# Experts' input stored as rows in halves, gate made in the experts' stage, an expert pair's y summed in one bank, nine weight blocks loaded early

## The chip, the cores and the metric

The kernel runs on one core of a Trainium2 chip. The metric is device time in microseconds (us) of one execution; lower is better. TensorE (PE) does the matmuls, VectorE (DVE), ScalarE (ACT) and GpSimd (POOL) the elementwise work, and SyncE (SP) issues the DMA transfers.

## What is computed

128 sequences of 128 tokens, width 256, run through four residual stages. Only the second one, a mixture of experts, and the LayerNorm ahead of it are touched by the change in what they do.

```python
x = x + cross_attention(layernorm(x), ctx)         # 16 heads of 16
x = x + ffn_moe(layernorm(x), Wg, bg, W1, b1, W2, b2)
x = x + attention2(ctx, ctx, layernorm(x), mask)   # 16 heads
x = x + spiking_ffn(layernorm(x))                  # 256 -> 1024 -> 256, 5 steps

def ffn_moe(x, ...):
    gate_logits = x @ Wg + bg                      # 8 experts
    top_vals, top_idx = top_k(gate_logits, 2)
    gate_scores = softmax(top_vals)                # per token
    for i in range(2):
        e = top_idx[..., i].reshape(-1)[:batch]    # one expert per sequence
        h = gelu(x @ W1[e] + b1[e])                # 256 -> 1024
        y = h @ W2[e] + b2[e]                      # 1024 -> 256
        out = out + gate_scores[..., i:i+1] * y
```

`reshape(-1)[:batch]` takes the first 128 entries, so all experts' numbers come from the 128 tokens of the first sequence: sequence b uses the two experts of token b of sequence 0.

## The kernel before

A unit is a pair of sequences (`PAIR` = 2), and there are 64 units. Products are made in f16 halves: every operand is a high part and a low part, and `three_passes` (L181) adds hi·hi, hi·lo and lo·hi, the matmuls of L183, L184 and L185. A shape like 128x512 in a row of a matmul is rows by columns of the result.

There are four phases, with a preparation of weights ahead of each. In a phase each engine runs its own list of `(lag, task)`, written out by hand: in step s, `run_steps` (L122) lets every task work on unit s − lag, in the order of the list, and an engine takes its instructions strictly in that order. The pieces of PSUM banks are shared out by a `plan` (lag, name) in the same order.

**Phase 1**, `attention(first=True)` (L470 to L1171): cross attention, then the LayerNorm for the experts. POOL makes the factors (`rstd1`: L397, L401, L412, L416), ACT applies them (`norm1`, L422), TensorE transposes the result (`t_1`, L449 in `transpose_pair`), ACT and DVE make its halves (`hi_h`, `lo_h`), and SP stores them column by column in `h_scratch` (`store_h`). TensorE makes the gate logits (`gate`, 14 matmuls of 8 columns), ACT copies them, DVE takes the largest (`top`); the experts' numbers of unit 0 are written to `idx_scratch` by SP once all units are done. From unit 32 on, every four units, SP loads one of four blocks (512 KB) of expert weights into `region` (`ahead`, L597). POOL's other tasks are `norm0` (factors L397, L401, then L440), `bias_x` (L771) and `maxima` (L744 to L749, small).

**Preparation of phase 2** (`prepare_experts`, L1240): 32 blocks of weights; ACT makes the high part of each (L1279), DVE the low part (L1285), from eight slots of raw blocks; the last six are done behind the shared heads' part (`prepare_shared_heads`). `gates` (L1174) makes the softmax of all gates at once.

**Phase 2**, `experts` (L1311): a unit has 8 chunks n (which sequence a, which of its two experts, which half of the hidden width). `up(n)` makes 4 groups of 128 hidden columns with 2 x 3 matmuls of 128 columns each (L183 to L185); `down(n − 3)` makes 4 steps j, in each one matmul of 512 columns (L1466: the high part of the hidden values against both halves of W2 side by side) and one of 256 (L1468: the low part against the high half). An expert's result thus stands in one bank of 512 columns as two sums, which DVE adds with two further operations (`add`, L1558, four per sequence). Between up and down ACT applies gelu (L1495) and DVE splits (L1513, L1516).

The expert's number is a value in a register, read from memory at the start of each unit on every engine that needs it (`read`, L1306), and each address that depends on it is computed by register instructions of the engine's sequencer, ahead of the matmul. In the profile these are `FUSED_REGOPS` and `ALU_OP` on PEldq, the read is `TENSOR_LOAD`. The lines of `down`:

```python
for j in range(4):
    row = w["w2"][:, bass.ds(e, 1), 4 * half + j, :, :].rearrange("p o t n -> p (o t n)")
    pe.matmul(o[:, :], hh[n % NH][:, j, :], row, start=half == 0 and j == 0, stop=False, ...)
    m = pe.matmul(o[:, 0:D], hl[n % NH][:, j, :], row[:, 0:D], start=False, stop=half == 1 and j == 3, ...)
```

**Phase 3**, `attention(first=False)`: the same function, second attention. It stores its LayerNorm as rows in halves (`rows1`, L430 and L433 in `split_rows`, on POOL) and **phase 4**, `spiking` (L1693), reads them with a transposing DMA (`columns_in`, L461 to L463). Phase 3's `ahead` loads late weights.

Of the kernel before, what the change touches and what calls it, by code (L numbers as in the profile page):

```python
# [36 lines left out]
P = 128  # L37
# [17 lines left out]
M_X = 15  # L55
KEPT = 3e38
# [143 lines left out]
def constants(k):  # L200
# [6 lines left out]
    c["minus_half"] = k.sb("minus_half", [P, PAIR], F32)  # L207
    s = k.sem("s_const")
# [3 lines left out]
    def gpsimd(g):  # L212
# [8 lines left out]
        g.memset(c["minus_half"][:, :], -0.5)  # L221

# [247 lines left out]
def attention(nc, k0, c, w, io, n_seq, first, glog_top=None, idx_d=None, raw_ahead=()):  # L470
# [9 lines left out]
    with ExitStack() as ctx:  # L480
# [22 lines left out]
        hT = first and two("hT", [P, 2, KB, PAIR * S], F16)  # L503
        hr = first or two("hr", [P, PAIR, 2, D], F16)
        gl = two("gl", [P, PAIR, EXP], F32)
        g8 = two("g8", [P, PAIR, EXP], F32)
        i8 = k.sb("i8", [P, EXP], U32)
# [24 lines left out]
        s_y2, s_yh, s_yl, s_o, s_x1, s_t1, s_hh, s_hl = (g(n) for n in "s_y2 s_yh s_yl s_o s_x1 s_t1 s_hh s_hl".split())  # L532
        s_g, s_gl, s_g8, s_gt = g("s_g"), g("s_gl"), g("s_g8", PAIR), g("s_gt")
        s_cut, s_x = ({n: g(f"s_{what}{n}") for n in cut_by} for what in ("cut", "under"))
        s_xb, s_hrh, s_hr = g("s_xb"), g("s_hrh"), g("s_hr")
        s_idx, s_idxd, s_late = k.sem("s_idx"), k.sem("s_idxd"), k.sem("s_late")

        if first:
            plan = [(10, "t_1"), (7, "y1"), (3, "v"), (8, "o"), (2, "t_x"), (7, "t_y"), (10, "gate"), (2, "q"),
                    (1, "t_c"), (6, "y0"), (2, "k"), (4, "t_max")]  # L540
            shared = (("t_1", "t_x", "y0", "t_max"), ("y1", "v", "t_y", "t_c"), ("o", "gate", "q", "k"))
# [39 lines left out]
        with nc.Block() as block:  # L581
            @block.sync
            def _(sp):
# [35 lines left out]
                def store_h(u):  # L619
                    if not first:  # L620
                        s_hr.wait(sp, u)
                        d_h.inc(rows_out(sp, h_out[u.no], hr[u.slot][:, :, :, :]), u)
                        return
                    s_hl.wait(sp, u)
                    s_hh.wait(sp, u)
# [1322 lines left out]
```

## Time and profile before

| | us |
|---|---|
| median of 3 executions | 3932.9 (3925.84 to 3933.43) |
| the profiled execution | 3932.82 |
| its span in the trace | 3930.9 |
| phase 1, first to last L401 of the first norm | 28.0 to 909.7 |
| phase 2, first to last read of the experts' numbers | 1039.1 to 2418.4 |
| phase 4's first load | 3244.5 |

| engine | busy us | share of the span | instructions |
|---|---|---|---|
| PE | 3732.9 | 95% | 47650 |
| PEld | 2907.6 | 74% | 47650 |
| DVE | 3129.4 | 80% | 5333 |
| ACT | 2251.2 | 57% | 4658 |
| POOL | 1879.8 | 48% | 2866 |

PE is a matmul, PEld the load of its stationary operand, which overlaps it. Ends of matmuls are modelled: a busy PE is not one at its peak. Register instructions and reads (PEldq) are not counted as busy; they have start times of their own in the trace. A row gives the line of the program, the engine, the operation, the tile written and those read, and how many; then durations in ns (min/median/max) and the first and last start in us.

### The profile page before, as it was taken

How to read it: one execution, taken by the hardware profiler on the slowest of the kernel's cores; microseconds unless marked ns; L12 is line 12 of the kernel's file. 1: busy time of each engine (PE TensorE's matmuls, PEld its weight loads, DVE VectorE, ACT ScalarE, POOL GpSimd, SP SyncE). 2: the span in 40 equal slices, each digit the busy share in tenths (PEclk: the TensorE clock that was granted, in tenths of full speed). 3: DMA queues.
4: the chain of work that ended last, by engine and by line, in shares of the span. 5: the costliest groups of instructions: out<-in, count | busy, mean ns of one | idle time of the engine just before them, and what ended most of it. 6: DMA issues, size and time to landing. Idle time of an engine off the chain costs nothing. (4 is left out here: it accounts for less than half of the span.)

```text
span 3930.9 us, 134664 instructions
## 1 busy us (share of the span) xinstructions
PE 3732.9 (95%) x47650; PEld 2907.6 (74%) x47650; DVE 3129.4 (80%) x5333; ACT 2251.2 (57%) x4658; POOL 1879.8 (48%) x2866
## 2 busy tenths in 40 slices
PE   5999999998499999999999997899999989999999
PEld 4788888886377777777777775466666658888888
DVE  4899998997777777777777775699888976777777
ACT  3777777776544444444444443577667764555554
POOL 4555555553133332222222223366666666777776
PEclk9999999999699999999999998899999999999999
DMA  4666666664522222222222223699999962233232
GB/s 118 184 193 193 199 200 200 192 193 126 192 77 84 77 80 64 73 67 70 73 64 76 62 75 78 152 214 212 203 218 212 217 151 71 73 79 76 73 81 68
DMA packets 766624, 502.33 MB, mean 128 GB/s; under 512 B 194421, under 2 KB 740408, under 8 KB 765864
## 3 DMA queue, kind: packets, MB, share of 16 engines
q1 hardware_dynamic: 765064, 493.22, 47.8%
q8 instruction: 420, 6.88, 0.8%
q14 instruction: 212, 1.74, 0.2%
q0 software_dynamic: 928, 0.49, 0.1%
HBM read 268.05 MB, written 214.96 MB: 123 GB/s over the span
## 5 line engine op out<-in xcount | busy, mean ns | idle before, releaser
L1495 ACT ACTIVATE phase_loop_hf<-phase_loop_hid,phase_b1T 128x128 f32<-128x128 f32 x2048 | 586.0, 368 | 706.1 <-PE phase_loop_hid L185 677.0
L183 PE MATMUL phase_loop_hid<-phase_loop_moe_h,phase_w_hi 128*128 128x128 f16 x4096 | 728.6, 220 | 12.0 <-DMA phase_loop_moe_h<-h_scratch 12.0
L185 PE MATMUL phase_loop_hid<-phase_loop_moe_h,phase_w_lo 128*128 128x128 f16 x4096 | 726.7, 219 | 0.0
L184 PE MATMUL phase_loop_hid<-phase_loop_moe_h,phase_w_hi 128*128 128x128 f16 x4096 | 726.7, 219 | 0.0
L1131 DVE TENSOR_REDUCE phase_loop_mx<-phase_loop_score 128x8 f32<-128x1024 f32 x512 | 625.5, 1222 | 102.7 <-PE phase_loop_score L868 92.1
L1466 PE MATMUL phase_loop_moe_y<-phase_w,phase_loop_hh 128*128 x2048 | 693.6, 379 | 1.1
L1468 PE MATMUL phase_loop_moe_y<-phase_w,phase_loop_hl 128*128 x2048 | 558.2, 273 | 0.0
L1042 ACT ACTIVATE phase_loop_pt<-phase_loop_scoreT 128x1024 f32<-128x1024 f32 x448 | 459.2, 1025 | 169.6 <-PE phase_loop_scoreT L902 169.2
L183 PEld LDWEIGHTS phase_loop_hid<-phase_loop_moe_h,phase_w_hi 128*128 x4096 | 400.7, 98 | 86.4 <-issue 12.3
L397 POOL TENSOR_SCALAR phase_loop_ln0b_ve<-phase_loop_ln0b_mv 128x2 f32<-128x2 f32 x64 | 23.1, 361 | 918.4 <-DVE phase_loop_ln0b_mv L390 918.4
L1513 DVE TENSOR_SCALAR phase_loop_hh<-phase_loop_hf 128x512 f16<-128x512 f32 x512 | 259.2, 506 | 250.2 <-PE phase_loop_moe_y L1468 196.8
L1516 DVE SCALAR_TENSOR_TENSOR phase_loop_hl<-phase_loop_hf,phase_loop_hh 128x512 f16<-128x512 f32 x512 | 411.4, 804 | 17.6
L184 PEld LDWEIGHTS phase_loop_hid<-phase_loop_moe_h,phase_w_hi 128*128 x4096 | 401.6, 98 | 5.7
L1827 POOL TENSOR_TENSOR phase_loop_sp_q<-phase_loop_sp_r 128x512 f32<-128x512 f32 x256 | 330.7, 1292 | 155.7 <-ACT phase_loop_sp_r L1798 155.7
L185 PEld LDWEIGHTS phase_loop_hid<-phase_loop_moe_h,phase_w_lo 128*128 x4096 | 400.7, 98 | 0.1
L1782 PE MATMUL phase_loop_sp_yb<-all_region,phase_loop_sp_fh 128*128 128x256 f16 x2048 | 349.2, 273 | 1.3 <-POOL phase_loop_sp_fl L1733 1.3
L1466 PEld LDWEIGHTS phase_loop_moe_y<-phase_w,phase_loop_hh 128*128 128x128 f16 x2048 | 200.2, 98 | 190.6 <-issue 4.1
L933 PE MATMUL phase_loop_av<-phase_loop_pt,phase_loop_vx 128*32 128x128 f32 x8192 | 332.6, 280 | 3.3 <-ACT phase_loop_pt L1042 3.2
L1798 ACT ACTIVATE phase_loop_sp_r<-phase_loop_sp_hid 128x512 f32<-128x512 f32 x256 | 153.1, 598 | 317.7 <-PE phase_loop_sp_hid L185 301.4
L1851 DVE SCALAR_TENSOR_TENSOR phase_loop_sp_cnt<-phase_loop_sp_y,phase_loop_sp_cnt 128x512 f32<-128x512 f32 x256 | 320.4, 1252 | 8.8
L183 PE MATMUL phase_loop_sp_hid<-phase_loop_sp_h,all_region 128*128 128x256 f16 x1024 | 280.4, 274 | 15.0 <-DMA phase_loop_sp_h<-h_scratch 15.0
L184 PE MATMUL phase_loop_sp_hid<-phase_loop_sp_h,all_region 128*128 128x256 f16 x1024 | 280.5, 274 | 0.0
(255 smaller groups left out, 9421.2 us busy)
## 6 DMA issues: line engine op xcount, KB each, us to landing
qk_scratch<-phase_loop_qk SPq DMA_DIRECT2D x192, 256.0 KB, 3.2
phase_loop_qS<-qk_scratch SPq DMA_DIRECT2D x768, 64.0 KB, 3.0
phase_loop_cin<-in_ctx SPq DMA_DIRECT2D x128, 256.0 KB, 4.2
x_scratch<-phase_loop_x SPq DMA_DIRECT2D x128, 256.0 KB, 3.7
phase_loop_kS<-qk_scratch SPq DMA_DIRECT2D x384, 64.0 KB, 2.5
ks_scratch<-ct_scratch SPq DMA_DIRECT2D x384, 64.0 KB, 2.4
phase_loop_kS<-ks_scratch SPq DMA_DIRECT2D x128, 192.0 KB, 3.9
phase_loop_xin<-in_x SPq DMA_DIRECT2D x64, 256.0 KB
```

The lines of the kernel that those rows point to most:

```text
L183: eng.matmul(out, l_hi, r_hi, start=start, stop=False)
L184: eng.matmul(out, l_hi, r_lo, start=False, stop=False)
L185: return eng.matmul(out, l_lo, r_hi, start=False, stop=stop)
L933: m = pe.matmul(av_bank[32 * j:32 * j + 32, ch * S:(ch + 1) * S], vx[u.slot4][:, a, 2 * b + hh, :], pt[n % len(pt)][:, hh * CH + j, :], st ...
L1042: act.activation(pt[n % len(pt)][:, :, :], score_t_bank[:, :].rearrange("p (j n) -> p j n", j=HB2), ACT.Exp, scale=exp_scale).then_inc(s_e ...
L1131: v.tensor_reduce(to, score_bank[:, :].rearrange("p (h j n) -> p h j n", h=2, j=CH), AX.X, ALU.max).then_inc(s_mx.sem, 1)
L1466: pe.matmul(o[:, :], hh[n % NH][:, j, :], row, start=half == 0 and j == 0, stop=False, skip_group_check=True)
L1468: m = pe.matmul(o[:, 0:D], hl[n % NH][:, j, :], row[:, 0:D], start=False, stop=half == 1 and j == 3, skip_group_check=True)
L1495: i = act.activation(hf[n % NF][:, j, :], hid_bank[n % 4][:, j * S:(j + 1) * S], ACT.Gelu, bias=w["b1"][:, bass.ds(e * HB + (4 * half + j) ...
L1516: v.scalar_tensor_tensor(out=hl[n % NH][:, :, :], in0=hf[n % NF][:, :, :], scalar=p2(H_X), in1=hh[n % NH][:, :, :], op0=ALU.mult, op1=ALU. ...
L1782: m = pe.matmul(o, l[n % 4][:, j, at], rr[:, hb, :], start=st and i == 0, stop=sto and i == 2, skip_group_check=True)
L1827: g.tensor_tensor(q[n][:, :, :], r[n][:, :, :], r[n][:, :, :], ALU.mult).then_inc(s_q.sem, 1)
```

## The change

- Phase 1 no longer makes h in columns. `rows1` runs on POOL in this phase too, right behind `rstd1` of the same unit, and `store_h` stores rows. `t_1`, `hi_h`, `lo_h`, `gate`, `copy_gate` and `top` are gone, and all five task lists and the banks' plans of the phase are written in another order. Nine weight blocks, not four, are loaded ahead, every three units (phase 3's late loads follow the same divisor). Nothing is written to `idx_scratch` at the end.
- The preparation reads the first unit's h with a transposing load, makes its gate logits, finds the experts' numbers after nine low parts and writes them to `idx_scratch` before block 26. It has 13 slots. `gates` is gone.
- Phase 2 reads h with `columns_in`, makes the gate logits of each unit on TensorE at the unit's start (`gate_logits`), their two largest on DVE behind the first split (`top`), and the softmax on POOL in five small operations (`gates`, two of them powers).
- In `down` each j has three matmuls of 256 columns, all into the same 256 columns; both experts of a sequence have the two halves of one bank. DVE adds twice per sequence, not four times. Several buffers move to a part of `region`.

```diff
-                        o = y_bank[a][ex]
+                        o = y_bank[a][:, ex * D:(ex + 1) * D]
                         for j in range(4):
                             row = w["w2"][:, bass.ds(e, 1), 4 * half + j, :, :].rearrange("p o t n -> p (o t n)")
-                            pe.matmul(o[:, :], hh[n % NH][:, j, :], row, start=half == 0 and j == 0, stop=False,
-                                      skip_group_check=True)
-                            m = pe.matmul(o[:, 0:D], hl[n % NH][:, j, :], row[:, 0:D], start=False,
-                                          stop=half == 1 and j == 3, skip_group_check=True)
+                            high, low = hh[n % NH][:, j, :], hl[n % NH][:, j, :]
+                            pe.matmul(o, high, row[:, 0:D], start=n % 4 == 0 and j == 0, stop=False, skip_group_check=True)
+                            pe.matmul(o, high, row[:, D:2 * D], start=False, stop=False, skip_group_check=True)
+                            m = pe.matmul(o, low, row[:, 0:D], start=False, stop=n % 4 == 3 and j == 3, skip_group_check=True)
...
-                tasks = [(1, read), (2, read_last)]
+                def gate_logits(u):
+                    d_h.wait(pe, u)
+                    s_gl.wait(pe, u.back(1))
+                    gate_products(pe, gate_bank, late, c, hT[u.slot]).then_inc(s_g.sem, 1)
+
+                tasks = [(1, read), (2, read_last), (1, gate_logits)]
...
-                        for i in range(4):
-                            ex, part = i // 2, i % 2
...
+                        for ex in range(2):
...
-                run_steps(g, [(2, factors), (2, rows), (2, bias), (2, halves)], units, 3)
+                run_steps(g, [(1, gates), (2, factors), (2, rows), (2, bias), (2, halves)], units, 3)
...
-                    d_h.inc(sp.dma_start(hT[u.slot][:, :, :, :], io["h"][u.no]), u)
+                    d_h.inc(columns_in(sp, hT[u.slot][:, :, :, :], io["h"][u.no]), u)
...
-                    tasks = [(9, rstd1), (2, norm0), (3, bias_x), (4, maxima)]
+                    tasks = [(6, bias_x), (8, maxima), (5, norm0), (12, rstd1), (12, rows1)]
...
-                    tasks = [(4, score(0)), (6, av(0)), (10, make["t_1"]), (7, make["y1"]), (6, av(1)), (4, score(1)),
...
+                    tasks = [(3, make["t_x"]), (8, make["t_y"]), (7, av(2)), (5, score(3)), (7, score_t(3)),
...
-                    n, at = divmod(u.no - units // 2, 4)
-                    if n not in range(4) or at:
+                    n, at = divmod(u.no - units // 2, 3)
+                    if n not in range(len(raw_ahead) if first else 4) or at:
...
+            if i == len(jobs) - LAST:
+                sp.wait_ge(s_gv, 3)
+                sp.dma_start(idx_d, which[0:idx_d.shape[0], 0:2]).then_inc(s_id, 16)
+                sp.wait_ge(s_id, 16)
+                sp.dma_start(listed[:, :, :], idx_d.rearrange("(o u a) n -> o u (a n)", o=1, a=PAIR)).then_inc(s_i, 16)
...
-        low(v, range(len(jobs) - LAST))
+        low(v, range(EARLY))
+        v.wait_ge(s_gp, 1)
+        v.tensor_scalar(logits[:, :], gate_bank[:, 0:EXP], p2(-LN_X - W_X), None, ALU.mult).then_inc(s_gv, 1)
+        v.wait_ge(s_gv, 1)
+        v.max(best[:, :], logits[:, :]).then_inc(s_gv, 1)
+        v.wait_ge(s_gv, 2)
+        v.max_index(which[:, :], best[:, :], logits[:, :]).then_inc(s_gv, 1)
+        low(v, range(EARLY, len(jobs) - LAST))
```

Here is TensorE's program in phase 2, the last trio of an up and the first step of the down behind it, before. ISA is the form of register instruction that the profile calls FUSED_REGOPS, REGISTER_ALU is its ALU_OP; `w` is the experts' weights, `hh` and `hl` the hidden values' halves.

```order
L183 ISA
L183 MATMUL phase_loop_hid<-phase_loop_moe_h,phase_w_hi 128x128
L184 MATMUL phase_loop_hid<-phase_loop_moe_h,phase_w_hi 128x128
L185 REGISTER_ALU
L185 MATMUL phase_loop_hid<-phase_loop_moe_h,phase_w_lo 128x128
L1466 ISA
L1466 MATMUL phase_loop_moe_y<-phase_w,phase_loop_hh 128x512
L1468 MATMUL phase_loop_moe_y<-phase_w,phase_loop_hl 128x256
```

And the same place now (the lines of `three_passes` are one further down, `hh` and `hl` stand in `region`):

```order
L184 ISA
L184 MATMUL phase_loop_hid<-phase_loop_moe_h,phase_w_hi 128x128
L185 MATMUL phase_loop_hid<-phase_loop_moe_h,phase_w_hi 128x128
L186 REGISTER_ALU
L186 MATMUL phase_loop_hid<-phase_loop_moe_h,phase_w_lo 128x128
L1452 ISA
L1452 MATMUL phase_loop_moe_y<-phase_w,all_region 128x256
L1453 ISA
L1453 MATMUL phase_loop_moe_y<-phase_w,all_region 128x256
L1454 MATMUL phase_loop_moe_y<-phase_w,all_region 128x256
```

A step j of down has one register instruction and 768 columns in two matmuls before, and two register instructions and the same 768 columns in three matmuls now. Over the program TensorE has 6144 ISA before and 8192 now, and 4096 REGISTER_ALU in both.

This is POOL's program in phase 1, one step, before:

```order
L401 TENSOR_TENSOR phase_loop_ln1a_rs<-phase_loop_ln1a_ve,all_minus_half 128x2
L412 TENSOR_SCALAR phase_loop_ln1a_nm<-phase_loop_ln1a_mv 128x2
L416 TENSOR_TENSOR phase_loop_ln1a_nb<-phase_loop_ln1a_nm,phase_loop_ln1a_rs 128x2
L397 TENSOR_SCALAR phase_loop_ln0a_ve<-phase_loop_ln0a_mv 128x2
L401 TENSOR_TENSOR phase_loop_ln0a_rs<-phase_loop_ln0a_ve,all_minus_half 128x2
L440 TENSOR_SCALAR phase_loop_ln0a_xn<-phase_loop_xin,phase_loop_ln0a_mv,phase_loop_ln0a_rs 128x256 x2
L771 TENSOR_TENSOR phase_loop_xin<-phase_loop_xin,phase_bo_b 128x512
L744 TENSOR_SCALAR phase_loop_nm<-phase_loop_mx 128x32
```

And now:

```order
L401 TENSOR_SCALAR phase_loop_ln1a_ve<-phase_loop_ln1a_mv 128x2
L405 TENSOR_TENSOR phase_loop_ln1a_rs<-phase_loop_ln1a_ve,all_minus_half 128x2
L416 TENSOR_SCALAR phase_loop_ln1a_nm<-phase_loop_ln1a_mv 128x2
L420 TENSOR_TENSOR phase_loop_ln1a_nb<-phase_loop_ln1a_nm,phase_loop_ln1a_rs 128x2
L434 CAST phase_loop_hr<-phase_loop_ln1a_xn 128x2x256
L437 TENSOR_TENSOR phase_loop_hr<-phase_loop_ln1a_xn,phase_loop_hr 128x2x256
L761 TENSOR_TENSOR phase_loop_xin<-phase_loop_xin,phase_bo_b 128x512
L734 TENSOR_SCALAR phase_loop_nm<-phase_loop_mx 128x32
```

L434 reads ln1a_xn, which ACT makes from the nb of L420, the instruction just ahead of it on POOL. Behind the two new operations stand the bias and the maxima of later steps.

## Rows read from the trace of the kernel before

**Rows 1.** Stretches: us, busy PE, PEld, DVE, ACT, POOL (x count), PEclk, DMA, GB/s

```profile
150.00:900.00 750.00, 748.70 (x11717) 604.19 (x11707) 675.68 (x1383) 551.11 (x906) 393.31 (x798) 1.00 0.66 195
1100.00:2350.00 1250.00, 1249.03 (x14850) 989.17 (x14848) 976.96 (x1857) 594.03 (x1972) 349.19 (x509) 1.00 0.24 72
```

**Rows 2.** First phase, line L401: ns min/median/max, first to last start, forms

```profile
L401 POOL TENSOR_TENSOR phase_loop_ln0a_rs<-phase_loop_ln0a_ve,all_minus_half x64: 712/713/725, 28.0 to 909.7; 128x2 f32<-128x2 f32 x64
```

**Rows 3.** First phase, TensorE, lines L449 and L185, one unit

```profile
L449 PE MATMUL phase_loop_ring<-all_ident,phase_loop_ln1a_xn x4: 272/273/328, 500.7 to 501.0; 128*128 128x128 f32 x4
...
L185 PE MATMUL phase_loop_ring<-phase_wg_hi,phase_loop_hT x4: 166/166/167, 507.6 to 507.9; 128*128 128x8 f16 x4
```

**Rows 4.** POOL groups, one period, 509.8:524.1; busy, mean ns, idle before, releaser

```profile
L744 POOL TENSOR_SCALAR phase_loop_nm<-phase_loop_mx 128x32 f32<-128x32 f32 x2 | 0.6, 301 | 7.8 <-DVE phase_loop_mx L1131 7.8
...
L397 POOL TENSOR_SCALAR phase_loop_ln1a_ve<-phase_loop_ln1a_mv 128x2 f32<-128x2 f32 x1 | 0.2, 191 | 1.2 <-DVE phase_loop_ln1a_mv L390 1.2
```

**Rows 5.** Third phase's last units: POOL L430, L433 and ACT L422

```profile
L430 POOL CAST phase_loop_hr<-phase_loop_ln1b_xn x2: 608/608/609, 3237.1 to 3238.9; 128x512 f16<-128x512 f32 x2
...
L433 POOL TENSOR_TENSOR phase_loop_hr<-phase_loop_ln1b_xn,phase_loop_hr x2: 1151/1152/1152, 3237.8 to 3239.7; 128x512 f16<-128x512 f32 x2
...
L422 ACT ACTIVATE phase_loop_ln1b_xn<-phase_loop_x,phase_loop_ln1b_nb,phase_loop_ln1b_rs x2: 584/592/599, 3237.2 to 3237.7; 128x256 f32<-128x256 f32 x2
```

**Rows 6.** Last norm factor of a phase, and first work or load behind it

```profile
L416 POOL TENSOR_TENSOR phase_loop_ln1a_nb<-phase_loop_ln1a_nm,phase_loop_ln1a_rs x2: 194/194/195, 974.1 to 976.8; 128x2 f32<-128x2 f32 x2
...
L1279 ACT ACTIVATE phase_w_hi<-all_region x8: 1040/1056/1058, 988.1 to 1030.2; 128x1024 f16<-128x1024 f32 x8
...
L416 POOL TENSOR_TENSOR phase_loop_ln1b_nb<-phase_loop_ln1b_nm,phase_loop_ln1b_rs x1: 196/196/196, 3236.9 to 3236.9; 128x2 f32<-128x2 f32 x1
...
L463 SPq DMA_TRANSPOSE phase_loop_sp_h<-h_scratch x2: 1256/1274/1292, 3244.5 to 3245.8; - x2
```

**Rows 7.** Preparation, DVE line L1285: first, last, and those around the break

```profile
L1285 DVE SCALAR_TENSOR_TENSOR phase_w_lo<-all_region,phase_w_hi x8: 1211/1226/1226, 990.0 to 1031.8; 128x1024 f16<-128x1024 f32 x8
...
L1285 DVE SCALAR_TENSOR_TENSOR phase_w<-prep_expert_raw,phase_w x8: 1216/1224/1226, 995.7 to 1037.5; 128x1024 f16<-128x1024 f32 x8
...
L1285 DVE SCALAR_TENSOR_TENSOR phase_w<-all_region,phase_w x2: 1216/1221/1226, 1025.2 to 1033.0; 128x1024 f16<-128x1024 f32 x2
```

**Rows 8.** Second phase's first matmuls, and the fourth phase's after a transposing load

```profile
L183 PEldq FUSED_REGOPS  x64: 46/46/46, 1041.7 to 1059.6; - x64
...
L183 PE MATMUL phase_loop_sp_hid<-phase_loop_sp_h,all_region x3: 393/421/421, 3248.3 to 3249.6; 128*128 128x256 f16 x3
```

**Rows 9.** Reads of the experts' numbers by TensorE's sequencer, whole run

```profile
L1306 PEldq TENSOR_LOAD <-phase_idx x65: 782/817/1016, 1039.1 to 2418.4; - x65
```

**Rows 10.** L183, the first chunk of a unit, then the second

```profile
L183 PEldq FUSED_REGOPS  x8: 46/46/46, 1320.2 to 1321.8; - x8
...
L183 PE MATMUL phase_loop_hid<-phase_loop_moe_h,phase_w_hi x8: 219/223/228, 1320.5 to 1322.0; 128*128 128x128 f16 x8
...
L183 PEldq FUSED_REGOPS  x8: 46/46/46, 1322.6 to 1324.5; - x8
...
L183 PE MATMUL phase_loop_hid<-phase_loop_moe_h,phase_w_hi x8: 219/219/219, 1323.5 to 1324.7; 128*128 128x128 f16 x8
```

**Rows 11.** Register instructions of up (L185) and of down (L1466) in one chunk

```profile
L185 PEldq ALU_OP  x8: 32/32/32, 1301.3 to 1303.0; - x8
...
L1466 PEldq FUSED_REGOPS  x4: 46/46/60, 1300.6 to 1301.0; - x4
```

**Rows 12.** Page, groups: down's two matmuls

```profile
L1466 PE MATMUL phase_loop_moe_y<-phase_w,phase_loop_hh 128*128 x2048 | 693.6, 379 | 1.1
L1468 PE MATMUL phase_loop_moe_y<-phase_w,phase_loop_hl 128*128 x2048 | 558.2, 273 | 0.0
```

**Rows 13.** POOL line L404, norm factors in the second phase

```profile
L404 POOL TENSOR_TENSOR phase_loop_ln0b_rv<-phase_loop_ln0b_ve,all_minus_half x64: 722/1175/1178, 1076.0 to 2427.6; 128x2 f32<-128x2 f32 x64
```

**Rows 14.** One stretch of the third phase, columns as in rows 1

```profile
2805.00:2810.00 5.00, 5.00 (x45) 3.38 (x45) 1.63 (x3) 2.51 (x4) 2.14 (x4) 0.50 1.17 179
```

More of the change, by code:

```diff
@@ L55 @@
 M_X = 15
+AHEAD = 9
 KEPT = 3e38
@@ L502, in attention @@
         x1 = two("x1", [P, PAIR, D], F32)
[L503 to L507, printed above, removed]
+        hr = two("hr", [P, PAIR, 2, D], F16)
         qkd = [nc.dram_tensor(f"qk_scratch{int(first)}{i}", (4, D, PAIR * S), F16, kind="Internal").ap() for i in range(2)]
@@ L619, in store_h @@
                 def store_h(u):
[L620 to L625, printed above, removed]
-                    d_h.inc(sp.dma_start(h_out[u.no], hT[u.slot][:, :, :, :]), u)
+                    s_hr.wait(sp, u)
+                    d_h.inc(rows_out(sp, h_out[u.no], hr[u.slot][:, :, :, :]), u)
                 def store_ct(u):
@@ L1171, in _, with gate_products @@
                 run_steps(v, tasks, units, DEPTH)
-def gates(kk, top, gate, n_seq):
-    e, d = kk.sb("gate_e", [P, n_seq], F32), kk.sb("gate_d", [P, n_seq], F32)
-    s = kk.sem("s_gate")
-    def vector(v):
-        v.tensor_tensor(d[:, :], top[:, :, 1], top[:, :, 0], ALU.subtract).then_inc(s, 1)
-        v.wait_ge(s, 2)
-        v.tensor_scalar(d[:, :], e[:, :], 1.0, None, ALU.add).then_inc(s, 1)
-        v.wait_ge(s, 3)
-        v.reciprocal(d[:, :], d[:, :]).then_inc(s, 1)
-        v.wait_ge(s, 4)
-        v.tensor_scalar(gate[:, :, 0], d[:, :], p2(-H_X - W_X), None, ALU.mult).then_inc(s, 1)
-        v.wait_ge(s, 5)
-        v.tensor_tensor(gate[:, :, 1], gate[:, :, 0], e[:, :], ALU.mult)
-    def scalar(act):
-        act.wait_ge(s, 1)
-        act.activation(e[:, :], d[:, :], ACT.Exp).then_inc(s, 1)
-    return {"vector": vector, "scalar": scalar}
+def gate_products(pe, bank, w, c, hT):
+    hi, lo = w["wg"]
+    for a in range(PAIR):
+        out = bank[:, a * EXP:(a + 1) * EXP]
+        at = slice(a * S, (a + 1) * S)
+        for kb in range(KB):
+            three_passes(pe, out, hT[:, 0, kb, at], hT[:, 1, kb, at], hi[:, kb, :], lo[:, kb, :], kb == 0, False)
+        m = pe.matmul(out, c["ones10"][:, 0:S], w["bg"][:, :], start=False, stop=True)
+    return m
 def late_views(region):
@@ L1308, in read_experts, with experts @@
     return values
-def experts(nc, k0, c, w, late, io, n_seq, gate):
+def experts(nc, k0, c, w, late, io, n_seq, spare):
     units = n_seq // PAIR
@@ L1530, in weight, with top @@
                 def weight(u, a, ex):
-                    return gate[:, bass.ds(u.no * PAIR + a, 1), ex]
+                    return gate[u.slot][:, a, ex:ex + 1]
+                def top(u):
+                    s_g.wait(v, u)
+                    s_gates.wait(v, u.back(2))
+                    settle(v, ln.ticks_v)
+                    v.tensor_scalar(gl[u.slot][:, :, :], gate_bank[:, 0:PAIR * EXP].rearrange("p (a n) -> p a n", a=PAIR),
+                                    p2(-LN_X - W_X), None, ALU.mult).then_inc(s_gl.sem, 1)
+                    s_gl.wait(v, u)
+                    for a in range(PAIR):
+                        v.max(g8[u.slot][:, a, :], gl[u.slot][:, a, :]).then_inc(s_g8.sem, 1)
                 def add_bias(a):
@@ L1910, in build @@
                 kk = Kit(nc, tmp, "prep2", k2)
-                most, rest = prepare_experts(kk, c, w, io, idx_d, first_raw, s_first)
-                together(nc, gates(kk, top, gate, n_seq), most, prepare_shared_heads(kk, c, w_late, io), rest)
-            experts(nc, k2, c, w, w_late, io, n_seq, gate)
+                most, rest = prepare_experts(kk, c, w, w_late, io, idx_d, first_raw, s_first)
+                together(nc, most, prepare_shared_heads(kk, c, w_late, io), rest)
+            experts(nc, k2, c, w, w_late, io, n_seq, region[:, 4 * HID:AHEAD * HID])
             k2.end_phase()
```

172 lines of the change are left out of this document (86 added, 86 removed).

## The prediction

> **What bounds the kernel now.** First I read the busy times of two long stretches [rows 1]. TensorE is busy for 748.70 of 750 us in the first phase and for 1249.03 of 1250 in the experts' (second) phase, at a granted clock of 1.00, the upper of its two levels (2.4 GHz). VectorE follows with 675.68 and 976.96. So both phases seem to be TensorE's. But a busy PE is a modelled number, and next I asked what hands TensorE its work.
>
> In the experts' phase each address depends on a number read at run time, so register instructions stand between the matmuls. Read the starts. In the first chunk of a unit the eight L183 matmuls start from 1320.5 to 1322.0 us, 1.5 / 7 = 0.21 us apart; in the next chunk from 1323.5 to 1324.7, 0.17 apart [rows 10]. A trio (L183 to L185) of 128-column matmuls can thus go in 0.17 us, and in the first chunk it does not. In that chunk the sequencer's own register instructions (PEldq) are as far apart as the matmuls: eight from 1320.2 to 1321.8, 0.23 each. With one more (ALU_OP) in each trio, eight of which take 1301.3 to 1303.0, 0.24 each [rows 11], a register instruction costs the sequencer about **0.12 us**. In down, four of them stand from 1300.6 to 1301.0, 0.13 apart though two matmuls lie between each pair [rows 11]: the register instruction is the price, the matmuls pass for nothing.
>
> Now count a unit. The reads of the experts' numbers stand (2418.4 - 1039.1) / 64 = **21.55 us** apart [rows 9], 0.9 us of which is the read (817 ns, and the way to the next instruction). The sequencer handles 8 chunks of 16 + 4 = 20 register instructions: 160 x 0.12 = 19.2, and 0.9, and some 1.4 of waits and hiccups. TensorE's arithmetic needs 24 x 0.057 (a third of 0.17) in up. In down the 512-column matmul lasts 379 ns and the 256-column one 273 [rows 12], an 8-column one 166 [rows 3]: the columns cost about 0.213 and 0.107, together 0.32 per j and 1.28 per chunk. The sum is 2.65 per chunk, 21.2 per unit. **Sequencer and arithmetic are level, and there is no slack in the sequencer.** That is the finding on which the forecast hangs.
>
> **The change, part by part.** The profiled execution took 3932.82 us (its span is 3930.9), the median of the runs is 3932.9, so the sum starts from 3932.8.
>
> *First phase.* TensorE loses the transposes of h (four L449 matmuls from 500.7 to 501.0, 0.5 with the last one's own time) and the gate (14 matmuls of 8 columns from 507.5, the last of the L185 kind starting at 507.9, 0.4) [rows 3]. A unit takes (909.7 - 28.0) / 63 = 14.00 us now [rows 2], TensorE-bound, so 13.1 after: 64 x 0.9 = 57.6, taken as **-57**. ACT and DVE only lose work here. POOL gains rows1: 0.61 for the cast and 1.15 for the subtraction [rows 5] with some 0.2 between; and, since it stands right behind rstd1 of the same unit, the wait for ACT's norm1: factor done at 3237.1 (3236.9 [rows 6] and 0.2), xn done at 3237.7 + 0.6 = 3238.3 [rows 5], 1.2 us. POOL now idles 7.8 / 2 + 1.2 = 5.1 of 14.0 us [rows 4] (the 7.8 counts two units). Occupied: 8.9 + 2.0 + 1.2 = 12.1 of 13.1. It fits by 1.0 us; what is queued behind the wait is bias_x and maxima, for which there are two or more steps of lag. Cost 0.
>
> *Phase ends.* From the last norm factor to the first work of the preparation: 988.1 - 976.8 = 11.3 us, through transposes, hi, lo, gate and the write and wait for the experts' numbers. In the third phase, which stores rows as the change does, from factor to the next phase's load are 3244.5 - 3236.9 = 7.6 [rows 6]. With 0.6 for what lies between load and work: **-3**.
>
> *Preparation.* DVE makes 32 low parts; the first starts at 990.0, the last ends at 1037.5 + 1.2 = 1038.7: 48.7 us. Between the 26th, which ends at 1025.2 + 1.2 = 1026.4, and the 27th at 1031.8 stand 5.4 us for the shared heads; the last six take 1038.7 - 1031.8 = 6.9, or 1.15 each, while the 26 before, which had to wait for their blocks, took 1026.4 - 990.0 = 36.4, or 1.40 each [rows 7]. With nine blocks ahead and thirteen slots I expect the pace of the last six: 32 x 1.15 + 5.4 + 0.6 for the first unit's top = 42.8. Between no gain and -7 (no addition for the top), taken at **-6**, since the blocks that waited are the ones now ahead. The first h comes by a transposing load beside this, and the experts' numbers are written before block 26.
>
> *Start of the second phase.* From the read at 1039.1 [rows 9] to the first instruction at 1041.7 [rows 8] are 2.6 us. A transposing load takes longer: issue at 3244.5 [rows 6], matmul at 3248.3 [rows 8], 3.8. That is +1.2, and +0.4 for the gate ahead of the first chunk [rows 3], less what the sequencer does meanwhile: **+1.5**. Later units load two units ahead, which hides it.
>
> *Gate in the unit.* 14 matmuls, 0.4 us of arithmetic per unit, no register instructions. Where the sequencer is the bound TensorE has holes for them: 0; where not, 64 x 0.4 = 26. POOL's five small operations hold two powers of up to 1.18 us [rows 13]; with the rest about 3 us per unit, beside the 349.19 / 1250 x 21.55 = 6.0 of now [rows 1]. They start after chunk 0 and are wanted after chunk 5, 12 us later: 0. The row shows the same power at 0.71 us in the first phase [rows 2] and 1.18 here: something holds POOL up. The Trainium skill (SBUF — State Buffer, section "SBUF: two separate sides") says that GpSimd and VectorE share a port pair as an exclusive lock, which would fit the row and leave the sum as it is; no trace here tells it from other causes.
>
> *Down.* Per j one 512-column and one 256-column matmul become three of 256. The columns are the same, 2 x 0.107 for 0.213: 0. But the sequencer now computes an address for the second matmul too: 8 rather than 4 register instructions per chunk, 32 more in a unit. At 0.118 (half of 0.236) that is 3.8 us per unit, and the sequencer had nothing left: 21.55 + 3.75 = **25.3**, so 64 x 3.75 = **+240**. Lower bound: the shortest chunk, 1322.6 - 1320.2 = 2.4 [rows 10], eight times, + 0.9 + 3.8 + 0.2 = 24.1, +163. Upper: every register instruction at the present mean, (21.55 - 0.9) / 160 = 0.129, 192 of them + 0.9 + 0.4 for the gate = 26.1, +291. DVE loses two of four adds per sequence there, and is far from the bound.
>
> Third and fourth phase: late weight loads stand three units apart, not four; one such load costs a hole and a stretch at half clock (0.50 [rows 14]), and their number stays four: 0.
>
> Sum: 3932.8 - 57 - 3 - 6 + 1.5 + 240 = 4108.3, forecast **4108**.
>
> **The rivals.** *A, the sequencer has slack:* the extra register instructions hide in the instruction queue or in matmuls that wait anyway. For it: TensorE is busy 1249.03 of 1250 [rows 1] and matmuls without a register instruction between them pass for nothing. Against: the trios 0.21 apart. It decides if an extra instruction costs below some 0.03 us. Then the phase gains only the gate's 26, and 3932.8 - 64.5 + 26 = **3894**, faster. The Trainium skill (TensorE: Matmul & The Clock Gate, section "Wait — 56ns, not 53.3ns?") has a fixed 2.5 ns for each further matmul and a floor of 25 ns; it counts no register instruction, and by it the split would cost 5 us in all. The trace does not agree for this stream: 0.21 us against 0.17. The same page's section "Back-to-back issue gap" has 131 ns for sustained 512-column matmuls, by which the split alone would add an estimated 2048 x (2 x 0.109 - 0.131) = 178 us; the row has 213 ns [rows 12], so that price is not there. *B, POOL bounds the first phase:* rows1 waits for ACT, which stands in another activation of up to 1 us, and POOL's loop needs 12.1 + 1.7 = 13.8 us instead of 13.1. It decides from an extra wait of 1.0. Then +0.7 x 64 = +45: **4152**. *C, the clock falls* in the new holes, as it did at 0.50 [rows 14]; if one unit in ten runs at 1.2 GHz, 42.4 us instead of 25.3, that is 6.4 x 17.1 = +109: **4217**. *D, half of the price hides*, +120: **3988**, or the change does not do what it says.
>
> **Chances.** Forecast 0.75, A 0.08, B 0.10, C 0.03, D 0.02, and 0.02 for a price just large enough to eat the gains. Range 4030 to 4160, from the bounds (4031 to 4159 by the lower and upper unit), which hold B too; A, C and D are left out. A measurement here tells some 0.2% (8 us) from no change. Faster 0.08 (A), same 0.02 (that last case), slower 0.90.
>
> **What would show it.** The reads of the experts' numbers 25.3 us apart, not 21.55; trios some 0.24 apart in every chunk, down's register instructions doubled to 4096, still 0.12 apart; a PE share in the second phase below 1249 of 1250. L401's first-phase starts 13.1 apart (B: 13.8). The low parts of the preparation done in 43, not 48.7. A unit near 21.9 would make the forecast wrong, and A right.

## The result, and the profile after

The changed kernel takes 4154.2 us (median of 4, 4151.92 to 4155.98) against 3933.2 of the kernel before: a ratio of 1.0566, 95% interval 1.0547 to 1.0584, **221 us slower**. Forecast were 4108, with a range of 4030 to 4160.

The page of the profiled execution (its span is 4154.1 us), busy time, share and instructions, and the granted clock in 40 slices:

```profile
PE 3900.6 (94%) x49269; PEld 3097.8 (75%) x49456; DVE 3005.8 (72%) x5010; ACT 2199.1 (53%) x4529; POOL 2147.2 (52%) x3316
...
PEclk9999999987999999999999999799999998999999
```

The same two stretches as in [rows 1], in the columns named there; the first is 50 us shorter, as the first phase now ends sooner:

```profile
150.00:850.00 700.00, 698.30 (x10705) 555.97 (x10704) 622.40 (x1167) 513.16 (x796) 481.23 (x902) 1.00 0.74 212
1100.00:2350.00 1250.00, 1223.81 (x14547) 1005.58 (x14545) 768.06 (x1492) 487.28 (x1639) 390.82 (x667) 1.00 0.22 61
```

TensorE is still full in the first phase (698.30 of 700). In the second it has 1223.81 of 1250 where it had 1249.03, and nothing else in the stretch is near its limit: DVE 768.06, POOL 390.82. So TensorE has holes there. Of waits for another engine the profile lists none in the second stretch; its one entry is "issue", ahead of the gate's first matmul of a unit:

```profile
PE phase_loop_moe_gate L184 <- issue: 21.3, 48, 0.5
```

The lengths of the two loops, first to last start:

```profile
L405 POOL TENSOR_TENSOR phase_loop_ln0a_rs<-phase_loop_ln0a_ve,all_minus_half x64: 718/720/723, 27.6 to 853.8; 128x2 f32<-128x2 f32 x64
...
L1263 PEldq TENSOR_LOAD <-phase_idx x65: 798/817/1021, 979.4 to 2639.3; - x65
```

The first phase's unit is (853.8 - 27.6) / 63 = 13.11 us, where [rows 2] gave 14.00. The reads of the experts' numbers are (2639.3 - 979.4) / 64 = **25.94 us** apart, where [rows 9] gave 21.55. The spans, stretch by stretch (the sum is the difference of the spans, 4154.1 - 3930.9 = 223.2; before it 0.4 is gained ahead of the first start):

| stretch, us | before | after | change | forecast |
|---|---|---|---|---|
| first phase, first to last L401 / L405 of the first norm | 881.7 | 826.2 | -55.5 | -57 |
| from there to the first read of the experts' numbers | 129.4 | 125.6 | -3.8 | -9 |
| first to last read | 1379.3 | 1659.9 | +280.6 | +241.5 |
| last read to the end | 1512.5 | 1514.8 | +2.3 | 0 |

What fills the 25.94 us is seen in the first and second chunk of a unit, as in [rows 10]:

```profile
L184 PEldq FUSED_REGOPS  x8: 46/46/46, 1628.3 to 1630.0; - x8
...
L184 PE MATMUL phase_loop_hid<-phase_loop_moe_h,phase_w_hi x8: 216/227/228, 1628.4 to 1630.1; 128*128 128x128 f16 x8
...
L184 PEldq FUSED_REGOPS  x8: 46/46/46, 1631.4 to 1633.1; - x8
...
L184 PE MATMUL phase_loop_hid<-phase_loop_moe_h,phase_w_hi x8: 219/223/228, 1631.8 to 1633.2; 128*128 128x128 f16 x8
```

The eight FUSED_REGOPS of a chunk, one per trio, are 1.7 / 7 = 0.24 us apart in both chunks, and with the ALU_OP between them that is 0.12 per register instruction. In the kernel before, the first matmul of the second chunk started 0.9 us behind its register instruction (1323.5 and 1322.6 in [rows 10]), so there was work in store and the matmuls ran 0.17 apart. Now it starts 0.4 us behind (1631.8 and 1631.4), and the matmuls are 1.4 / 7 = 0.20 apart. Down, in the same unit:

```profile
L1452 PEldq FUSED_REGOPS  x4: 46/46/60, 1630.3 to 1631.1; - x4
...
L1453 PEldq FUSED_REGOPS  x4: 46/46/46, 1630.5 to 1631.2; - x4
...
L1452 PEldq FUSED_REGOPS  x2048: 46/46/60, 990.8 to 2643.2; - x187
```

L1452 and L1453 alternate, eight register instructions from 1630.3 to 1631.2, 0.12 to 0.13 each, where [rows 11] has four from 1300.6 to 1301.0. The last row counts the phase's: 2048, and L1453 has as many again.

### The profile page after: what moved, and what is told of

Its sections match the earlier page's. It is cut to its first block and busy times, and to the rows that moved or that the text cites. A ratio compares the mean times of both kernels' runs of the same rounds, so it can differ in the third digit from the quotient of the medians.

```text
span 4154.1 us, 140077 instructions
## 1 busy us (share of the span) xinstructions
PE 3900.6 (94%) x49269; PEld 3097.8 (75%) x49456; DVE 3005.8 (72%) x5010; ACT 2199.1 (53%) x4529; POOL 2147.2 (52%) x3316
## 5 line engine op out<-in xcount | busy, mean ns | idle before, releaser
L1485 ACT ACTIVATE all_region<-phase_loop_hid,phase_b1T 128x128 f32<-128x128 f32 x2048 | 584.5, 368 | 1006.6 <-PE phase_loop_hid L186 1005.1
L184 PE MATMUL phase_loop_hid<-phase_loop_moe_h,phase_w_hi 128*128 128x128 f16 x4096 | 841.3, 224 | 3.2
L186 PE MATMUL phase_loop_hid<-phase_loop_moe_h,phase_w_lo 128*128 128x128 f16 x4096 | 824.8, 219 | 0.0
L185 PE MATMUL phase_loop_hid<-phase_loop_moe_h,phase_w_hi 128*128 128x128 f16 x4096 | 824.7, 219 | 0.0
L1503 DVE TENSOR_SCALAR all_region<-all_region 128x512 f16<-128x512 f32 x512 | 287.5, 561 | 592.1 <-ACT all_region L1485 589.6
L1452 PE MATMUL phase_loop_moe_y<-phase_w,all_region 128*128 x2048 | 562.5, 275 | 3.6 <-issue 0.4
L1453 PE MATMUL phase_loop_moe_y<-phase_w,all_region 128*128 x2048 | 562.7, 275 | 0.0
L1454 PE MATMUL phase_loop_moe_y<-phase_w,all_region 128*128 x2048 | 558.2, 273 | 0.0
L1828 POOL TENSOR_TENSOR phase_loop_sp_q<-phase_loop_sp_r 128x512 f32<-128x512 f32 x256 | 351.4, 1373 | 133.9 <-ACT phase_loop_sp_r L1799 133.9
L185 PEld LDWEIGHTS phase_loop_hid<-phase_loop_moe_h,phase_w_hi 128*128 x4096 | 402.9, 98 | 5.0
L1506 DVE SCALAR_TENSOR_TENSOR all_region<-all_region 128x512 f16<-128x512 f32 x512 | 359.2, 702 | 17.6
L184 PE MATMUL phase_loop_sp_hid<-phase_loop_sp_h,all_region 128*128 128x256 f16 x1024 | 280.2, 274 | 14.6 <-DMA phase_loop_sp_h<-h_scratch 14.6
L185 PE MATMUL phase_loop_sp_hid<-phase_loop_sp_h,all_region 128*128 128x256 f16 x1024 | 280.2, 274 | 0.0
L186 PE MATMUL phase_loop_sp_hid<-phase_loop_sp_h,all_region 128*128 128x256 f16 x1024 | 280.2, 274 | 0.0
```

What stands on the lines that cost most here:

```text
L184: eng.matmul(out, l_hi, r_hi, start=start, stop=False)
L185: eng.matmul(out, l_hi, r_lo, start=False, stop=False)
L186: return eng.matmul(out, l_lo, r_hi, start=False, stop=stop)
L1452: pe.matmul(o, high, row[:, 0:D], start=n % 4 == 0 and j == 0, stop=False, skip_group_check=True)
L1453: pe.matmul(o, high, row[:, D:2 * D], start=False, stop=False, skip_group_check=True)
L1454: m = pe.matmul(o, low, row[:, 0:D], start=False, stop=n % 4 == 3 and j == 3, skip_group_check=True)
```

## The experiments

Ten kernels ran. In the first seven the question is what in the second phase costs the time.

**One split alone.** The kernel before, with the one matmul of 512 columns made as two of 256:

```diff
-pe.matmul(o[:, :], hh[n % NH][:, j, :], row, start=half == 0 and j == 0, stop=False, ...)
+pe.matmul(o[:, 0:D], hh[n % NH][:, j, :], row[:, 0:D], start=half == 0 and j == 0, stop=False, ...)
+pe.matmul(o[:, D:2 * D], hh[n % NH][:, j, :], row[:, D:2 * D], start=False, stop=half == 1 and j == 3, ...)
```

> The kernel before, with only this of the change: the 512-column matmul of down is made as two of 256, each with an address of its own, into the same places as before (2048 more register instructions, 2048 more matmuls, same columns). If the sequencer's register instructions bound the second phase: 32 x 0.124 = 4.0 us more per unit and some 0.2 of hiccups, reads of the experts' numbers 25.7 us apart, in all 3933 + 64 x 4.2 = 4202 us. If the rest of the change (gate in the unit, buffers in the region, one bank) had cost the time: 3933 to 3945.

Measured: 4201.47 us in one execution, beside 3927.86 for the kernel before (7 executions, 3925.94 to 3939.25). The reads:

```profile
L1306 PEldq TENSOR_LOAD <-phase_idx x65: 542/817/1019, 1037.4 to 2683.4; - x65
```

(2683.4 - 1037.4) / 64 = 25.72 us. The split is enough for 4.17 of the 4.39 us that the change adds to a unit, without the gate, the region or the bank. Whether the register instruction or the matmul costs, this run can't tell.

**The same matmuls, without the further register instruction.** Both 256-column matmuls read the same half:

```diff
-pe.matmul(o[:, D:2 * D], hh[n % NH][:, j, :], row[:, D:2 * D], start=False, ...)
+pe.matmul(o[:, D:2 * D], hh[n % NH][:, j, :], row[:, 0:D], start=False, ...)
```

> As the run before, but the second of the two 256-column matmuls reads the same high half of W2 as the first, so its address needs no register instruction (the low half of W2 is left out of the result). Again 2048 more matmuls, but as many register instructions as the kernel before. If register instructions are the price: 3933 to 3940, reads 21.5 to 21.7 apart. If each further matmul has a price on the sequencer or in TensorE: as the run before, 4200. By the Trainium skill's sustained figure for 512 columns (131 ns, TensorE: Matmul & The Clock Gate, Back-to-back issue gap), which the trace of before did not show, an estimated 178 us more than before: 4111.

Measured: 3937.15 us, one execution.

```profile
L1306 PEldq TENSOR_LOAD <-phase_idx x65: 578/817/1017, 1037.6 to 2420.7; - x65
...
L1466 PEldq FUSED_REGOPS  x2048: 46/46/60, 1048.2 to 2423.8; - x187
...
L1466 PE MATMUL phase_loop_moe_y<-phase_w,phase_loop_hh x2048: 272/273/282, 1048.3 to 2425.7; 128*128 x187
```

(2420.7 - 1037.6) / 64 = 21.61 us, 0.06 more than before for 32 further matmuls, 2 ns each. The pair of runs has the same number of matmuls and columns and differs by one register instruction per j: 25.72 - 21.61 = 4.11 us per unit, 0.128 each. **It is the register instruction.** The Trainium skill (TensorE: Matmul & The Clock Gate, section "Wait — 56ns, not 53.3ns?") gives a fixed 2.5 ns per further matmul; the 2 ns of these two traces agree. The same page of the Trainium skill, in its section "Back-to-back issue gap", has a sustained 131 ns for 512 columns, by which this run would take an estimated 4111 us; the 3937.15 measured do not agree with it.

**Two splits.** The other matmul of down is split as well, into 128 and 128 columns, so there are 12 register instructions per chunk:

```diff
-m = pe.matmul(o[:, 0:D], hl[n % NH][:, j, :], row[:, 0:D], ...)
+pe.matmul(o[:, 0:P], hl[n % NH][:, j, :], row[:, 0:P], ...)
+m = pe.matmul(o[:, P:D], hl[n % NH][:, j, :], row[:, P:D], ...)
```

> The kernel before with both of down's matmuls split, 256 + 256 and 128 + 128 columns, each part with an address of its own: 12 register instructions per chunk in down instead of 4 (the run with one split had 8), same columns. If the price is per register instruction and the sequencer is alone the bound: the same step again, 25.72 + 4.1 = 29.8 us per unit, 4201 + 64 x 4.1 = 4464 us. If the step from 4 to 8 was something else (a bank, an order): clearly less. If the clock falls in the longer holes: more, and a granted clock below 1.00 in the stretch.

Measured: 4466.18 us, one execution, beside 3930.44 for the kernel before.

```profile
L1306 PEldq TENSOR_LOAD <-phase_idx x65: 537/818/1018, 1037.7 to 2954.0; - x65
...
1100.00:2350.00 1250.00, 1215.70 (x13341) 918.37 (x13340) 712.22 (x1333) 421.38 (x1418) 245.27 (x380) 1.00 0.18 53
```

(2954.0 - 1037.7) / 64 = 29.94 us: 4.22 more than with one split, after 4.17 for the first. The price is linear, 0.13 us for each register instruction, and the granted clock stays at 1.00 with the holes in it. The same number comes out of whole units: less the 0.9 us of the read, (21.55 - 0.9) / 160 = 0.129 before, (25.72 - 0.9) / 192 = 0.129 with one split, (29.94 - 0.9) / 224 = 0.130 with two. So the kernel before lies on this line too: its unit was already the sequencer's.

**No register instruction at all, in both kernels.** Constants stand in for the experts' numbers on every engine, so the selection of experts is left out, and the reads go with the register instructions:

```diff
-at = idx[0:1, bass.ds(row, 1), cols].rearrange("p o n -> p (o n)")
-_, values = nc.values_load_multi_w_load_instructions(at, engines=[eng.engine], ...)
+values = [(c + 2) % EXP for c in range(cols.start, cols.stop)]
```

> The changed kernel with constants in place of the experts' numbers on every engine (the reads and the selection by the gate are left out; all matmuls, columns and other work stay). No register instruction is left in the second phase. If they were the bound: TensorE's arithmetic remains, 21.2 + 0.4 for the gate = 21.6 us per unit instead of 25.94, 4154 - 64 x 4.3 = 3877. If DVE, POOL's gates, ACT or the matmul count bound the unit: near 4154, or wherever that engine stops it (POOL some 10 us busy per unit, DVE 16).

> The kernel before with constants in place of the experts' numbers (reads and selection left out), so without a register instruction in the second phase; every matmul stays. If sequencer and arithmetic are level there, as the prediction says: 21.2 us per unit (the changed kernel without them had 21.54 with 0.35 for the gate), 3933 - 64 x 0.35 = 3910. If the sequencer had been well above the arithmetic before: 3890 or less. If below: 3933.

Measured: the changed kernel 3878.51 us, the kernel before 3908.08, one execution each. With no reads left, the unit is taken from what runs once in it: in the changed kernel DVE's copy of the gate's logits, in the kernel before the gelus (32 per unit), whose first and last starts are 1045.9 and 2419.3 with the reads.

```profile
L1495 ACT ACTIVATE phase_loop_hf<-phase_loop_hid,phase_b1T x2048: 347/368/412, 1045.9 to 2419.3; 128x128 f32<-128x128 f32 x187
...
L1525 DVE TENSOR_SCALAR phase_loop_moe_gl<-phase_loop_moe_gate x64: 164/167/168, 990.3 to 2344.6; 128x16 f32<-128x16 f32 x64
...
L1493 ACT ACTIVATE phase_loop_hf<-phase_loop_hid,phase_b1T x2048: 347/368/378, 1046.0 to 2392.9; 128x128 f32<-128x128 f32 x187
```

The first row is the kernel before with its reads, the other two are the runs without. (2344.6 - 990.3) / 63 = 21.50 us for the changed kernel. For the kernel before the gelus stretch over 2392.9 - 1046.0 = 1346.9 us instead of 1373.4, which scales 21.55 to 21.13. So without register instructions and reads a unit takes 21.13 us, near the 21.2 that the prediction had for TensorE's arithmetic, and 0.37 more with the gate: in the kernel before, the sequencer (21.55) stood 0.4 above it, about level as the prediction had it, and in the changed kernel 4.4 above. Without the numbers the changed kernel would be the faster one, by 30 us.

**Down as before, in the changed kernel.** The gate needs a PSUM bank, which is why this could not be had by undoing the lines: here the hidden values give one up, and down goes ahead of up in each chunk, so that its wait still guards the bank that up writes.

```diff
-hid_bank = [k.ps(f"hid{i}") for i in range(4)]
-y_bank = [k.ps(f"moe_y{a}") for a in range(PAIR)]
+hid_bank = [k.ps(f"hid{i}") for i in range(3)]
+def hid(u, n):
+    return hid_bank[(u.no * NC + n) % 3]
+y_bank = [[k.ps(f"moe_y{a}{ex}") for ex in range(2)] for a in range(PAIR)]
...
+tasks.append((1, down(n - 3, e_now)) if n >= 3 else (2, down(n + NC - 3, e_before)))
 tasks.append((1, up(n)))
-tasks.append((1, down(n - 3, e_now)) if n >= 3 else (2, down(n + NC - 3, e_before)))
```

> The changed kernel with down as before: 512 and 256 columns per j, one bank per sequence and expert, four adds; the banks come from the hidden values, which have three instead of four, with down put ahead of up in each chunk. Everything else of the change stays. Sequencer theory: 20 register instructions per chunk again, 21.55 us and 0.2 to 0.4 for the gate at the unit's start: 21.8 to 22.0 per unit, 4154 - 64 x 4.05 = 3895 (3885 to 3905), faster than before. Rival: with three banks up waits for gelu, or the gate and the rows' loads carry part of the loss: above 3933.

Measured: 3892.71 us (4 executions), 0.9906 of the kernel before, interval 0.9888 to 0.9924.

```profile
L1263 PEldq TENSOR_LOAD <-phase_idx x65: 538/817/1020, 980.1 to 2373.5; - x65
```

(2373.5 - 980.1) / 64 = 21.77 us. Everything else of the change is in this kernel: its gains in the first phase are kept, and it is 261 us faster than the changed kernel, with 2048 register instructions fewer. Against the kernel before it is 0.9% faster, small but clear of the interval.

**The gate's wait.** In the same kernel, TensorE's wait for the logits' copy of the unit before is left out; the order is kept by down's wait for a later split, which DVE makes after that copy.

```diff
 d_h.wait(pe, u)
-s_gl.wait(pe, u.back(1))
```

> The four-bank version without gate_logits' wait for DVE's copy of the gate bank of the unit before (the order is kept by down's wait for the split of a later chunk, which DVE makes after that copy). The wait stands in the trace as an instruction of its own (EVENT_SEMAPHORE) and the next one comes 0.165 us behind it. If each instruction that the sequencer handles is paid for: unit 21.77 - 0.16 = 21.6, 64 x 0.16 = 10 us less, about 3872 for the profiled execution's 3884. If TensorE's arithmetic (21.54 per unit without register instructions) has become the bound: 21.65 to 21.77.

Measured: 3886.94 us, one execution.

```profile
L1263 PEldq TENSOR_LOAD <-phase_idx x65: 540/817/1020, 980.4 to 2368.0; - x65
```

(2368.0 - 980.4) / 64 = 21.68, a gain of 0.09 and not of 0.16, and within the 21.65 to 21.77 of the second theory. That the arithmetic holds it there is not shown, though, and the traces point to another reason. From the read to the next register instruction it is 1.04 us (median) with this wait and 0.94 without it; in the kernel before, where nothing stands between the two, it is 0.88. So the wait costs the sequencer 0.10 us, about what the run gained, and the 0.165 of the expectation held the passing of the gate's matmuls as well.

The last three ask about the preparation, where the forecast had -6; in the four-bank version it takes 978.6 + 1.2 - 933.7 = 46.1 us.

**Numbers written earlier.**

```diff
+if i == 18:
+    sp.wait_ge(s_gv, 3)
+    sp.dma_start(idx_d, which[0:idx_d.shape[0], 0:2]).then_inc(s_id, 16)
 if i == len(jobs) - LAST:
-    sp.wait_ge(s_gv, 3)
-    sp.dma_start(idx_d, which[0:idx_d.shape[0], 0:2]).then_inc(s_id, 16)
     sp.wait_ge(s_id, 16)
```

> The four-bank version with the experts' numbers written before block 18 and waited for before block 26, where it wrote and waited before block 26. In the changed kernel's preparation SP stood 11 us in that wait and DVE 2.4 us for the numbers (L1252). If that wait is what the preparation lost of its forecast: DVE's wait for the numbers gone, preparation 2.4 to 3 us shorter (low parts from first start to last end 44.5, not 47.0). If the blocks' transfers set it (1.4 us per block): no gain, 47.

Measured: 3897.46 us, one execution. The low parts of it (first and last start; 1.2 us each):

```profile
L1236 DVE SCALAR_TENSOR_TENSOR phase_w_lo<-all_region,phase_w_hi x12: 1210/1220/1226, 939.1 to 984.0; 128x1024 f16<-128x1024 f32 x12
L1236 DVE SCALAR_TENSOR_TENSOR phase_w<-all_region,phase_w x12: 1210/1218/1226, 940.2 to 985.2; 128x1024 f16<-128x1024 f32 x12
```

985.2 + 1.2 - 939.1 = 47.3, not 44.5. DVE's wait for the numbers is gone (5.4 us between the 26th and 27th part, where the four-bank version has 6.3 and the changed kernel 7.9), but the 26 parts ahead took 35.0 us instead of 32.8. The run with both edits, below, has the same preparation: 5.4 us for the break too, 33.3 for the 26 parts, 45.6 in all. Neither reaches 44.5. But that number came from the changed kernel, where DVE's wait was 2.4 us; in the four-bank version it was only 0.9, and these two executions of the same preparation lie 1.7 apart. So the runs do not tell the two theories apart, and whether a wait removed here comes back as waits for blocks is not shown.

**Both edits.**

> Both edits together on the four-bank version: 3893 - 10 - 2.5 = 3880; 0.988 of the kernel before. Rival: neither shows, 3893.

Measured: 3886.57 us (4 executions), 0.9881 of the kernel before, interval 0.9865 to 0.9898. Against the four-bank version this is 6 us, within what the intervals leave open, where 12.5 were expected. The reads are 21.67 us apart, as in the run without the gate's wait (21.68); the three runs that keep it have 21.77 to 21.79.

**Four blocks ahead instead of nine**, on the four-bank version:

```diff
-if n not in range(len(raw_ahead) if first else 4) or at:
+if n not in range(4) or at:
...
-for i in range(len(first_raw), slots):
+for i in range(4, slots):
```

> The four-bank version with four blocks loaded ahead instead of nine, everything else alike. If the early blocks are what made the 26 low parts ahead of the shared heads shorter (36.4 us before, 32.3 after): preparation 4 us longer, 51. If the thirteen slots alone do it, since loads need not wait for free slots: 47.

Measured: 3897.45 us, one execution.

```profile
L1235 DVE SCALAR_TENSOR_TENSOR phase_w_lo<-all_region,phase_w_hi x12: 1216/1224/1226, 932.4 to 982.4; 128x1024 f16<-128x1024 f32 x12
L1235 DVE SCALAR_TENSOR_TENSOR phase_w<-all_region,phase_w x12: 1216/1224/1226, 933.5 to 983.5; 128x1024 f16<-128x1024 f32 x12
```

983.5 + 1.2 - 932.4 = 52.3 us against 46.1 of the four-bank version: the five further blocks are worth 6.2 us, 1.2 each, less than the 1.4 that one took in the kernel before (36.4 / 26). The first theory, and a little more than its 51. With thirteen slots and four ahead the preparation is even longer than the 48.7 of [rows 7].

## Why the prediction was right, and where its sizes were off

Measured are 4154, 46 us above the forecast and 6 below the upper end of the range, which held only just. The misses all point the same way: 39 us in the second phase, 5 between the phases, 1.5 and 2.3 in the rest. None cancelled another. The total alone would have been a poor witness, since rival B, with 4152, is nearer to it than the forecast; only the stretches tell the two apart.

**The finding holds.** The prediction took the level of sequencer and arithmetic from starts of register instructions, against a TensorE that seemed busy for all but 1 of 1250 us. Three pairs of runs show it: split with and without an address (4201 and 3937), first and second split (+4.17 and +4.22 us per unit), and both kernels without register instructions (21.13 and 21.50 against 21.55 and 25.94).

**Down, +240, measured +281 (with the start of the phase in it, +1.5): the term that was mis-sized.** The prediction priced a register instruction at 0.118 and took 3.75 per unit, where 4.39 were added. The run with one split has 4.17 of that, 0.130 per instruction. The 0.118 was half of a trio's 0.236, the mean of two kinds: the next register instruction stands 0.124 behind a FUSED_REGOPS and 0.112 behind an ALU_OP, and those added are all FUSED_REGOPS. The rest are gaps that are longer, up to 0.31 us, about one in eight in the kernel before, the changed one and those with one and two splits, so more instructions bring more of them. The prediction's own upper bound took the mean over a unit, 0.129, which holds these gaps; with 0.4 for the gate it gave 26.1, and 25.94 were measured.

**Gate, 0, measured about 0.2 per unit.** It is the remaining 25.94 - 25.72 = 0.22, and the four-bank version stands 0.22 above the kernel before as well. The prediction took 0 because TensorE has holes for the gate's matmuls. But they and a wait stand in the sequencer's way between the read and the next register instruction: 1.07 us there (mean) in the changed kernel, 0.88 with one split and no gate.

**First phase, -57, measured -55.5 over 63 units** (13.11 for 13.1). Rival B is out. POOL's new work and its wait for ACT, in one period:

```profile
L437 POOL TENSOR_TENSOR phase_loop_hr<-phase_loop_ln1a_xn,phase_loop_hr 128x512 f16<-128x512 f32 x1 | 1.2, 1164 | 0.2 <-POOL phase_loop_hr L434 0.2
...
L434 POOL CAST phase_loop_hr<-phase_loop_ln1a_xn 128x512 f16<-128x512 f32 x1 | 0.6, 609 | 1.5 <-issue 1.5
```

The cast starts after 1.5 idle us (estimated 1.2 for the norm; the profile names no releaser here), and POOL is busy 481.23 / 700 x 13.11 = 9.0 us of the 13.11. TensorE, at 698.30 of 700, is the bound as before.

**Ends and preparation, -9, measured -3.8.** The last norm factor is now made at 923.3 and the first work of the preparation starts at 930.9, 7.6 us for the former 11.3: -3.7, a little more than the -3 of the forecast, and the first low part follows 1.1 us later, not 1.9. But from the first norm's last start to that of the last norm it is now 922.1 - 853.8 = 68.3 us, for 65.9 before, a +2.4 that the forecast did not have. And the preparation came out at 47.0 and not 42.8, a gain of 1.7 for the 6 of the forecast:

```profile
L1235 DVE SCALAR_TENSOR_TENSOR phase_w_lo<-all_region,phase_w_hi x12: 1211/1217/1227, 932.0 to 976.7; 128x1024 f16<-128x1024 f32 x12
L1235 DVE SCALAR_TENSOR_TENSOR phase_w<-all_region,phase_w x12: 1215/1218/1225, 933.1 to 977.8; 128x1024 f16<-128x1024 f32 x12
...
L1252 DVE TENSOR_SCALAR phase_idx<-prep_experts_listed x1: 276/276/276, 966.8 to 966.8; 1x256 uint32<-1x256 uint32 x1
...
L1214 SPq DMA_DIRECT2D idx_scratch<-prep_first_which x1: 2173/2173/2173, 952.3 to 952.3; - x1
...
DMA to landing us min/median/max: 11.0/11.0/11.0
```

977.8 + 1.2 - 932.0 = 47.0. The 26 parts took 32.3 us, 1.24 each and not 1.15. Only nine of 32 blocks were there, and with five fewer the 26 parts took 38.5 us (the four-block run) for 32.8. And SP's write of the numbers landed 11.0 us after its issue, six blocks having been issued in the 8.4 us ahead of it; DVE then stood 2.4 us (L1252 at 966.8). In the kernel before, the same 1 KB was written with no block on its way, and landed in 3.1:

```profile
L709 SPq DMA_DIRECT2D idx_scratch<-phase_loop_i x1: 319/319/319, 983.0 to 983.0; - x1
...
DMA to landing us min/median/max: 3.1/3.1/3.1
```

The prediction counted the DMA as a step with no queue in front of it. How the two waits, for blocks and for the numbers, add up is open, as said above.

**Start of the second phase, +1.5, measured +0.8 as far as it can be read apart.** First read to first register instruction is 3.4 us, for 2.6 before:

```profile
L184 PEldq FUSED_REGOPS  x29: 46/46/46, 982.8 to 989.8; - x29
```

**Third and fourth phase, 0, measured +2.3.** The kernels of this study, which leave these phases alone but for the loads' divisor, differ by more among themselves (1508.2 in the four-bank version to 1517.1 without the gate's wait).

**Rivals.** A (the sequencer has slack, 3894) and D (half the price hides, 3988) fall with the pair of runs, B with the first phase's 13.11 us. C falls too: a granted clock of 1.00 in the second phase, even with two splits.

## What to carry to other kernels

An engine that is busy 99.9% by its matmuls can be fed by a sequencer that has no slack: where addresses depend on values read at run time, count the register instructions of a unit, multiply by their mean price over whole units (here 0.129 us; the 0.118 read off the closest ones was too low), and hold that against the arithmetic. Then, in a kernel like this one, a matmul with the same columns but one more such address is not free, and one that reads two neighbouring blocks through one address is the cheaper form. The four-bank version with both later edits keeps the change's other gains at 0.9881 of the kernel before, by paying for the gate's bank with one of the hidden values instead of with addresses.

## What was not expected of the hardware

- A register instruction of TensorE's queue lasts 46 ns (32 for ALU_OP) in the trace and costs 0.13 us of the sequencer's time (4.11 us per unit for 32 of them, between two runs with the same matmuls), and four with two matmuls between each pair stand 0.13 apart as well [rows 11]. Such a duration says nothing of the price; the spacing does, best as a mean over whole units.
- In the sequence of register instructions about every eighth gap is longer than 0.13, up to 0.31 us, before as after the change. What it is stays open; no run here varied it.
- A transfer of 1 KB issued behind 512 KB blocks took 11.0 us to land (9.9 in the early-write run); with none on its way, in the kernel before, it took 3.1. The queue is the likely reason; no run varied it alone.
- A wait that stands as an instruction of its own on TensorE's queue costs the sequencer about 0.10 us, a little less than a register instruction: 1.04 us from the read to the next register instruction with it and 0.94 without.
